# A four-block transformer stack on one core: a new table of stage times and PSUM banks, the instructions unchanged

## The chip, the core and the metric

The kernel runs on one core of a Trainium2 chip. It is a single program for the five engines: TensorE (PE) multiplies matrices and writes PSUM, VectorE (DVE) and ScalarE (ACT) read PSUM and SBUF, GpSimd (POOL) works on SBUF alone, and SyncE (SP) issues the DMAs. The metric is the device time of one execution in microseconds.

## The reference, cut to what matters

The input x is 64 rows of sequences with 64 positions and 128 features, that is 4096 tokens. Eight blocks follow each other, each added to x with a gate of its own:

```python
x = x + tanh(g_xattn[0]) * L0_xattn(ctx, layernorm(x), mask, ...)     # cross attention, 8 heads
x = x + tanh(g_ffn[0])   * L0_ffn(layernorm(x), ...)                  # two layers of local attention + gated MLP
x = x + tanh(g_xattn[1]) * L1_xattn(layernorm(x), ctx, lens, ...)     # linear + decayed "patches"
x = x + tanh(g_ffn[1])   * L1_ffn(layernorm(x), Wg, A, B)             # top 2 of 8 low-rank experts
x = x + tanh(g_xattn[2]) * L2_xattn(ctx, layernorm(x), mask, b)       # attention on given keys and values
x = x + tanh(g_ffn[2])   * L2_ffn(layernorm(x), ...)                  # ternary weights, 8-bit activations
x = x + tanh(g_xattn[3]) * L3_xattn(layernorm(x), ctx, ...)           # attention, 16 heads
x = x + tanh(g_ffn[3])   * L3_ffn(layernorm(x), ...)                  # ternary weights, conv of 3 taps, silu
```

All of it is per sequence, so that a tile of two sequences (128 tokens) goes through the whole stack without any other tile.

## The kernel before, in words

There are 32 tiles of 128 tokens. For one tile the work is a chain of some 250 **stages**, each a few instructions on one engine. A stage's name says where it is: `l0a` is the first cross attention, `l0f0` and `l0f1` the two layers of the first feed-forward block, `l1a`, `l1f`, `l2a`, `l2f`/`l2g`, `l3a` (with two halves `l3a0`, `l3a1`), `l3f`/`l3g` the others. The ending says what it does: on PE `_yt`, `_qt`, `_pt`, `_ot` are transposes, `_sc` scores, `_pv` weights times values, `_out` the last product; on ACT `_exp` is the exponential and `_ht`, `_pts`, `_ots`, `_qts` copy a transposed result from PSUM to SBUF; on DVE `_max` and `_sub` take the row maximum off the scores, `_st`, `_var`, `_eps`, `_y` are a layer norm, `_x` adds a block's result to x; on POOL `_rstd` is the power -1/2.

Several tiles are under way at once: most buffers exist G = 5 times and tile i uses number i mod 5. Each engine is a single queue, so the order in which stages of different tiles follow each other on an engine is fixed when the program is written. That order comes from the **table**. Every stage has a time in tenths of a microsecond; tile i's stage counts as that time plus PERIOD * i, with PERIOD = 489; `in_turn` (line 194) always takes the stage with the smallest such number among the next stages of all tiles:

```python
head = min(left, key=lambda h: (TIMES[h[0]][h[3]] + PERIOD * h[1], h[1]))
```

A tile's own stages on an engine keep their order whatever the table says, and every stage waits on semaphores for its inputs. So the table decides only who stands in front of whom. There are eight lists: PE, ACT, "patch" (two ACT stages, `patch_sq` on line 711 and `patch_power` on line 716), DVE, POOL, "pick" (two POOL stages, `pick_reach` with its powers and compares on lines 504 to 609, and `picks`), SP (the issues of DMAs: `*_dup`, `second`, `first`, `third`, `store`), and "prep" (DVE work on weights in the first tiles).

The second part is the **bank table**. PSUM has eight banks. Each PE stage has a first bank, a number of banks, and the stages that read it. `take` (line 1298) makes a PE stage wait for the readers of whatever lay in its banks before:

```python
for k in range(bank, bank + n):
    for reader, of in held.get(k, ()):
        stage_of(reader, of)
    held[k] = [(reader, i) for reader in readers]
```

`stage_of` (line 1285) leaves a wait out where PE has already waited for a later stage of the same engine, judged by the same table. So the number of waits on PE also follows from the table: writing out both orders gives 2,052 waits on PE before.

ACT loads a table of functions (line 696) whenever the next stage needs another set than the one loaded: the exponential is in one set, Gelu and tanh in the other. With the order before that is 71 loads, two per tile in the steady part.

Lines that the prediction speaks of: PE 1315 (transposes of 128x128, among them `l1f_ot` from `vtmp`, `l2a_yt`, `l0a_yt`), 1322 (four or eight transposes: `l3a0_pt`, `l3a1_pt`, `l3g_qt`), 1336 and 1344 (`l0a_sc`, `l2a_sc`), 1382 (`l0f_qk`), 1388 (`l0f1_v`, `l0f0_v`), 1395 (`l0f_qkt`), 1402 and 1408 (`l0f_sc`), 1455 to 1459 (`l0a_kv`), 1500 (`l1a_out`, second part), 1565 (`l3a_sc`). ACT 711 (`patch_sq`), 739 (`l3g_round` and other roundings), 761 (`l0f_sq`), 785 (`l2g_qts`, `l3g_qts`), 807 (`l1f_tanh`). DVE 989 (`_y`: from `xin` it is `l0a_y`), 1005 and 1008 (`_max`, `_sub`), 1025 (`l1a_x`), 1053 (`l0f_den`), 1059 and 1062 (`l0f_turned`), 1068 (`l0f_qkn`), 1177 (`l1f_o`, writes `vtmp`), 1182 (`l1f_x`), 1219 (`l3a_part`), 1116 (`l0a_st`). POOL 504 (powers and sums), 607 and 609 (`pick_reach`). SP 463 and 464 (`_dup`), 472 and 473 (`second`).

Of the kernel before, what the change touches and what calls it, by code (L numbers as in the profile page):

```python
# [42 lines left out]
PE_TIMES = """
    l0a_kv 695, l0a_yt 695, l0a_q 702, l0a_sc 785, l0a_pt 836, l0a_pv 851, l0a_ot 875, l0a_out 889, l0f0_yt 950,
    l0f0_qk 954, l0f0_v 1107, l0f0_qkt 1121, l0f0_sc 1157, l0f0_pt 1195, l0f0_pv 1244, l0f0_ot 1288, l0f0_wo 1309,
    l0f0_sh 1329, l0f0_lt 1378, l0f0_hid 1405, l0f0_out 1502, l0f1_yt 1521, l0f1_qk 1547, l0f1_v 1551,
    l0f1_qkt 1718, l0f1_sc 1750, l0f1_pt 1777, l0f1_pv 1796, l0f1_ot 1823, l0f1_wo 1844, l0f1_sh 1856, l0f1_lt 1889,
    l0f1_hid 1930, l0f1_out 1946, l1a_yt 2014, l1a_out 2014, l1f_yt 2031, l1f_lg 2047, l1f_ot 2142, l1f_out 2166,
    l2a_yt 2214, l2a_sc 2215, l2a_pt 2252, l2a_pv 2260, l2f_qt 2335, l2f_hid 2356, l2g_qt 2421, l2g_out 2437,
    l3a_yt 2493, l3a_qkv 2493, l3a0_sc 2510, l3a1_sc 2627, l3a0_pt 2658, l3a0_pv 2683, l3a1_pt 2704, l3a1_pv 2727,  # L50
    l3a_tt 2735, l3a_ot 2752, l3a_out 2768, l3f_qt 2835, l3f_hid 2867, l3g_qt 2953, l3g_out 2970
    """
ACT_TIMES = """
    l0a_vs 681, l0a_ht 684, l0a_exp 837, l0a_pts 837, l0a_ots 893, l0f0_hs 931, l0f0_sq 968, l0f0_vs 1112,
    l0f0_qts 1122, l0f0_exp 1170, l0f0_pts 1200, l0f0_ots 1301, l0f0_lts 1389, l0f0_bent 1449, l0f1_hs 1550,
    l0f1_sq 1566, l0f1_vs 1583, l0f1_qts 1727, l0f1_exp 1741, l0f1_pts 1781, l0f1_ots 1825, l0f1_lts 1882,
    l0f1_bent 1937, l1a_ht 2044, l1f_ht 2049, l1f_tanh 2112, l1f_ots 2127, l2a_ht 2203, l2a_exp 2227, l2a_pts 2227,
    l2f_round 2333, l2f_qts 2358, l2f_bent 2369, l2g_round 2391, l2g_qts 2431, l3a_ht 2484, l3a_q 2484, l3a_vs 2497,
    l3a0_exp 2606, l3a0_pts 2650, l3a1_exp 2663, l3a0_os 2687, l3a1_pts 2698, l3a1_os 2709, l3a_ots 2759,
    l3f_round 2825, l3f_qts 2856, l3f_bent 2870, l3g_round 2962, l3g_qts 2962  # L60
    """
# [3 lines left out]
DVE_TIMES = """
    l0a_st 532, l0a_var 575, l0a_eps 587, l0a_y 621, l0a_k 706, l0a_qs 731, l0a_max 792, l0a_sub 796, l0a_inv 868,
    l0a_o 871, l0a_x 886, l0f_st 902, l0f_var 904, l0f_eps 904, l0f_y 936, l0f0_den 1011, l0f0_turned 1026,
    l0f0_qkn 1090, l0f0_max 1136, l0f0_sub 1145, l0f0_inv 1242, l0f0_o 1263, l0f0_y1 1310, l0f0_st 1322,
    l0f0_var 1337, l0f0_eps 1346, l0f0_y 1364, l0f0_gated 1464, l0f0_x 1506, l0f1_den 1584, l0f1_turned 1588,
    l0f1_qkn 1670, l0f1_max 1760, l0f1_sub 1767, l0f1_inv 1791, l0f1_o 1796, l0f1_y1 1856, l0f1_st 1861,  # L70
    l0f1_var 1861, l0f1_eps 1863, l0f1_y 1907, l0f1_gated 1924, l0f1_x 1958, l1a_st 1966, l1a_var 1971,
    l1a_eps 1979, l1a_y 1997, l1a_x 2024, l1f_st 2024, l1f_var 2033, l1f_eps 2054, l1f_lgs 2077, l1f_top 2080,
    l1f_mid 2080, l1f_rest 2093, l1f_sel 2106, l1f_w 2121, l1f_o 2143, l1f_x 2160, l2a_st 2177, l2a_var 2180,
    l2a_eps 2186, l2a_y 2219, l2a_max 2219, l2a_sub 2230, l2a_inv 2262, l2a_o 2262, l2a_x 2265, l2f_st 2285,
    l2f_var 2294, l2f_eps 2301, l2f_y 2302, l2f_abs 2312, l2f_lim 2319, l2f_inv 2327, l2f_step 2362, l2f_pre 2367,
    l2g_abs 2397, l2g_lim 2403, l2g_inv 2406, l2g_step 2435, l2g_x 2453, l3a_st 2457, l3a_var 2467, l3a_eps 2471,
    l3a_y 2483, l3a_part 2495, l3a0_max 2545, l3a0_sub 2551, l3a1_max 2640, l3a1_sub 2685, l3a_inv 2742, l3a_o 2746,
    l3a_x 2769, l3f_st 2778, l3f_var 2787, l3f_eps 2792, l3f_y 2792, l3f_abs 2809, l3f_lim 2826, l3f_inv 2826,
    l3f_step 2830, l3f_q 2835, l3f_act 2896, l3g_abs 2896, l3g_lim 2905, l3g_inv 2931, l3g_step 2931, l3f_x 2976
    """  # L80
# [1641 lines left out]
```

## Time and profile before

| what | value |
|---|---|
| median of 3 runs | 1769.86 us (1769.22 to 1777.59) |
| the profiled execution, its own time | 1784.65 us |
| its span, first to last instruction | 1782.9 us |
| mean granted TensorE clock | 0.928 |
| PE busy | 1443.3 us, 81% |
| DVE busy | 1366.3 us, 77% |
| ACT busy | 980.0 us, 55% |
| POOL busy | 733.6 us, 41% |
| chain that ended last | PE 43%, DVE 30%, ACT 16%, issue 9% |

The chain that ended last goes back from the last instruction to whatever released each step. Its shares say that no engine alone sets the end: the chain changes between PE, DVE and ACT many times in each tile. The program is periodic: after the first four tiles the same sequence of instructions comes back with each tile, about 50 us apart, and so the profile is best read one period at a time, and in differences of period between tiles.

### The profile page before, as it was taken

The numbers are of one execution on the slowest core, as the hardware profiler recorded it, in microseconds if no ns is written. First come the engines' busy times: TensorE is split into PE (matmuls) and PEld (weight loads), VectorE is DVE, ScalarE is ACT, GpSimd is POOL, SyncE is SP. The second block draws the span as 40 slices with busy tenths as digits, with TensorE's granted clock in tenths as the row PEclk, the third lists the DMA queues.
The fourth block names the chain that finished last, engine by engine and source line by source line (L and its number), as shares of the span: only waits on it lengthen the run. The fifth ranks groups of instructions, "written<-read, shape, count | busy, mean of one in ns | idle before, by whom it ended". The sixth has DMA issues, their size and how long they took to land.

```text
span 1782.9 us, 41970 instructions
## 1 busy us (share of the span) xinstructions
PE 1443.3 (81%) x16268; PEld 1022.2 (57%) x16268; DVE 1366.3 (77%) x4055; ACT 980.0 (55%) x1992; POOL 733.6 (41%) x1140
## 2 busy tenths in 40 slices
PE   1567888888888888888888888888888888987775
PEld 1345565566665655666655556666566656665432
DVE  4466687887888888888887888888888888887652
...
DMA packets 130947, 64.34 MB, mean 36 GB/s; under 512 B 97591, under 2 KB 123575, under 8 KB 130494
## 3 DMA queue, kind: packets, MB, share of 16 engines
...
## 4 chain that ended last, share of the span: by engine, by line
PE 43%; DVE 30%; ACT 16%; issue 9%; POOL 1%; POOLq 0%; DVEq 0%; DMA 0%; SPq 0%; ACTq 0%
PE ps_all L1322 9%; DVE mx L1005 4%; PE ps_all L1315 4%; PE ps_all L1440 3%; PE ps_all L1356 3%; ACT wide_b L777 3%; DVE wide_b L1008 2%; ACT L696 2%; PE ps_all L1344 2%; PE ps_all L1426 2%; DVE den L1053 2%; DVE wide_b L1062 2%; PE ps_all L1395 2%; DVE wide_a L1059 2%; DVE small L1032 2%
## 5 line engine op out<-in xcount | busy, mean ns | idle before, releaser
L504 POOL TENSOR_TENSOR rstd<-rstd,minus_half 128x1 f32<-128x1 f32 x320 | 174.9, 550 | 944.3 <-DVE rstd L983 944.2
L1005 DVE TENSOR_REDUCE mx<-ps_all 128x8 f32<-128x1024 f32 (+1 forms) x192 | 165.9, 864 | 152.8 <-PE ps_all L1344 134.3
L504 POOL TENSOR_TENSOR rden<-rden,minus_half 128x16 f32<-128x16 f32 x64 | 188.0, 2937 | 9.7 <-issue 0.4
L504 POOL TENSOR_TENSOR wide_a<-wide_a,wide_b 128x256 f32<-128x256 f32 x256 | 177.5, 724 | 6.4 <-DVE wide_b L1062 6.4
L1322 PE MATMUL ps_all<-ident,wide_b 128*128 128x128 f32 x1024 | 170.6, 308 | 8.1 <-ACT wide_b L746 6.9
L733 ACT COPY wide_a<-ps_all 128x512 f32<-128x512 f32 (+1 forms) x192 | 136.6, 728 | 38.2 <-PE ps_all L1322 26.9
L1322 PEld LDWEIGHTS ps_all<-ident,wide_b 128*128 128x128 f32 x1024 | 143.9, 165 | 12.0 <-ACT wide_b L746 10.2
L733 ACT COPY wide_c<-ps_all 128x512 f32<-128x512 f32 (+1 forms) x96 | 69.9, 728 | 128.1 <-PE ps_all L1322 128.1
L696 ACT ACT_TABLE_LOAD x70 | 89.8, 1283 | 75.2 <-DVE wide_a L1202 47.1
L1382 PE MATMUL ps_all<-w_qkv,ht_shift 128*128 128x512 f32 x256 | 127.4, 622 | 2.2 <-ACT ht_shift L756 2.2
L1008 DVE TENSOR_TENSOR wide_b<-ps_all,mx 128x512 f32<-128x512 f32 (+1 forms) x160 | 125.8, 786 | 1.4
L746 ACT ACTIVATE wide_b<-wide_b 128x512 f32<-128x512 f32 (+1 forms) x160 | 114.6, 716 | 16.0 <-DVE wide_b L1008 11.3
L1440 PE MATMUL ps_all<-ht,w 128*128 128x128 f32 x768 | 99.3, 281 | 0.6 <-ACT ht L731 0.6
L733 ACT COPY ht<-ps_all 128x128 f32<-128x128 f32 x160 | 42.1, 263 | 101.8 <-PE ps_all L1315 100.9
L761 ACT ACTIVATE wide_c<-ps_all 128x1024 f32<-128x1024 f32 x64 | 65.5, 1024 | 55.9 <-PE ps_all L1382 55.9
L1440 PEld LDWEIGHTS ps_all<-ht,w 128*128 128x128 f32 x768 | 95.2, 199 | 0.9 <-issue 0.8
L1609 PE MATMUL ps_all<-w_conv,xt 128*64 128x512 f32 x384 | 94.2, 628 | 0.0
L1097 DVE SCALAR_TENSOR_TENSOR wide_a<-ps_all,b,wide_b 128x128 f32<-128x128 f32 x192 | 55.2, 343 | 50.8 <-ACT wide_b L777 50.8
L1315 PE MATMUL ps_all<-ident,vtmp 128*128 128x128 f32 x128 | 43.7, 341 | 56.9 <-DVE vtmp L1177 43.8
L1388 PE MATMUL ps_all<-w_qkv,ht_shift 128*128 128x512 f32 x128 | 69.2, 625 | 20.4 <-DVE wide_b L1008 20.4
L1068 DVE TENSOR_TENSOR wide_b<-wide_a,rden 128x1024 f32<-128x1024 f32 x64 | 77.9, 1217 | 9.8 <-POOL wide_c L665 6.6
L1053 DVE TENSOR_REDUCE den<-wide_c 128x16 f32<-128x1024 f32 x64 | 77.5, 1212 | 9.1 <-ACT wide_c L761 8.9
...
## 6 DMA issues: line engine op xcount, KB each, us to landing
...
wide_c<-wide_c SPq DMA_DIRECT2D x128, 64.0 KB, 2.3
...
```

Of the source, the lines that this page charges most:

```text
L504: return gp.tensor_tensor(o, a, b, op)
L696: a.preload_act_table_set(name)
L733: a.copy(to, of).then_inc(*done(name))
L746: a.activation(of[:, s, 0:width], of[:, s, 0:width], ACT.Exp, scale=scale).then_inc(*done(f"{n}_exp"))
L1005: v.tensor_reduce(most, of, AX.X, ALU.max).then_inc(*done(f"{n}_max"))
L1008: tt(to, of, bc(most, 3, of.shape[3]), ALU.subtract).then_inc(*done(f"{n}_sub"))
L1053: v.tensor_reduce(den[:, s, :], wide_c[:, s, 0:2 * BANK].rearrange("p (g e) -> p g e", g=16), AX.X, ALU.add).then_inc(*done(f"{n}_den"))
L1315: nc.tensor.transpose(ps(name, 0, P), of, ident[:]).then_inc(*done(name))
L1322: m = nc.tensor.transpose(ps(name, c * P, P), of[:, c * P:c * P + P], ident[:])
L1382: m = mm(ps(f"{n}_qk", q * BANK, BANK), hs, w_qkv[:, L, q * INNER:q * INNER + INNER], start=True, stop=True)
L1440: m = mm(ps(f"{n}_hid", half * BANK + c * P, P), w_1[:, L, half, c, :], ht[:, s, :], start=True, stop=True)
L1609: m = mm(ps_all[64 * b:64 * b + 64, BANKS["l3f_hid"][0], :], xt[:, s, b, tap:tap + ROW], w_conv[:, tap, :], start=False, stop=(tap == 2))
```

## The change

Every number of the eight lists of stage times is new, and so is nearly every bank of the bank table. PERIOD, the names of the stages, their order within a tile, what each stage does, the readers of each PSUM result and the set-up are the same. The parts of the diff that the prediction speaks of:

```diff
 PERIOD = 489
 PE_TIMES = """
-    l0a_kv 695, l0a_yt 695, l0a_q 702, l0a_sc 785, ...
-    l0f1_qk 1547, l0f1_v 1551, l0f1_qkt 1718, ... l1f_yt 2031, l1f_lg 2047, l1f_ot 2142, l1f_out 2166,
-    l2a_yt 2214, ... l3g_qt 2953, l3g_out 2970
+    l0a_kv 711, l0a_yt 780, l0a_q 834, l0a_sc 855, ...
+    l0f1_qk 1609, l0f1_v 1629, l0f1_qkt 1720, ... l1f_yt 2102, l1f_lg 2102, l1f_ot 2188, l1f_out 2196,
+    l2a_yt 2247, ... l3g_qt 3022, l3g_out 3029
 ACT_TIMES = """
-    ... l0f0_sq 968, ... l3g_round 2962, l3g_qts 2962
+    ... l0f0_sq 1042, ... l3g_round 2982, l3g_qts 2999
 PATCH_TIMES = """
-    patch_sq 0, patch_power 1162
+    patch_sq 499, patch_power 1260
 DVE_TIMES = """
-    ... l0a_y 621, ... l0f0_sub 1145, ... l1f_o 2143, ... l3a1_max 2640, l3a1_sub 2685, ...
+    ... l0a_y 812, ... l0f0_sub 1286, ... l1f_o 2248, ... l3a1_max 2752, l3a1_sub 2760, ...
 POOL_TIMES = """
-    l0a_rstd 537, l0a_part 584, ...
+    l0a_rstd 574, l0a_part 698, ...
 PICK_TIMES = """
-    pick_reach 551, picks 1247
+    pick_reach 442, picks 1563
 SP_TIMES = """
-    l0a_dup 733, l0f0_dup 1019, l0f1_dup 1760, second 2219, first 2250, third 2411, store 3003
+    l0a_dup 0, l0f0_dup 459, l0f1_dup 642, second 1295, first 1299, third 1525, store 2202
 BANK_TABLE = """
-l0f1_v 2 1 l0f1_vs
+l0f1_v 5 1 l0f1_vs
-l3a0_sc 1 2 l3a0_sub
+l3a0_sc 3 2 l3a0_sub
-l0a_q 0 1 l0a_qs
+l0a_q 4 1 l0a_qs
 ...
```

Written out with `in_turn`, one period of the new order on PE reads (the number behind a stage is how many tiles back it is; before, `l1f_ot-3` stood in front of `l0a_kv`, `l3g_qt-4` in front of `l0f0_out-1`, and `l0f1_qkt-2` behind `l3a0_pv-4`):

```
l0a_kv l1f_ot-3 l1f_out-3 l3a0_pt-4 l0f1_qkt-2 l3a0_pv-4 l0f0_pt-1 l3a1_pt-4 l2a_yt-3 l0a_yt l2a_sc-3
l3a1_pv-4 l0f0_pv-1 l0a_q l3a_tt-4 l0f1_sc-2 l2a_pt-3 l0a_sc ... l2g_qt-3 l0f0_qk l2g_out-3 l0f1_out-2
l0f0_out-1 l3g_qt-4 l3a_yt-3 l3g_out-4 l3a_qkv-3 l1a_yt-2 l0f1_yt-1 l1a_out-2 l3a0_sc-3 l0f1_qk-1
l1f_yt-2 l1f_lg-2 l0f1_v-1 l0f0_v l0f0_qkt l0f0_sc l3a1_sc-3
```

The part of the order on DVE, before and after:

```
before: l1a_x-2 l1f_st-2 ... l3a0_max-3 l3a0_sub-3 l0f0_qkn l0f1_den-1 l1f_lgs-2 l0f1_turned-1 l1f_top-2
        l1f_mid-2 l0a_y+1 l1f_rest-2 l1f_sel-2 l0f0_max l1f_w-2 l0f0_sub l1f_o-2 l3a1_max-3 l0f1_qkn-1
        l1f_x-2 l0a_k+1 l2a_st-2 l2a_var-2 l2a_eps-2 l3a1_sub-3 l0a_qs+1 l2a_y-2
after:  l1a_x-2 l0a_st+1 l1f_st-2 ... l3a0_max-3 l3a0_sub-3 l0f0_qkn l1f_lgs-2 l0f1_den-1 l1f_top-2
        l0f1_turned-1 l1f_mid-2 l1f_rest-2 l1f_sel-2 l1f_w-2 l0f0_max l1f_o-2 l3a1_max-3 l0f0_sub
        l0f1_qkn-1 l3a1_sub-3 l1f_x-2 l2a_st-2 l2a_var-2 l2a_eps-2 l2a_y-2 l0a_y+1 l0a_k+1
```

With the new order PE has 2,260 waits in place of 2,052, and ACT again 71 table loads.

## Rows read from the trace of the kernel before

**Rows 1.** PE timeline: first instruction of `l0a_kv` in tiles 4, 11, 12, 31.

```profile
211.29 0.32 PE L1455 MATMUL ps_all<-rows,row_sel 128*128 128x128 bf16 x1
...
566.58 0.22 PE L1455 MATMUL ps_all<-rows,row_sel 128*128 128x128 bf16 x1
...
615.13 0.22 PE L1455 MATMUL ps_all<-rows,row_sel 128*128 128x128 bf16 x1
...
1568.77 0.31 PE L1455 MATMUL ps_all<-rows,row_sel 128*128 128x128 bf16 x1
```

**Rows 2.** Windows of PE: stretch, us, PE busy (x), PEclk, DMA share, GB/s.

```profile
566.60:615.10 48.50, 41.52 (x509) 1.00 0.14 37
...
965.00:1016.90 51.90, 44.24 (x509) 0.95 0.13 34
...
611.00:614.90 3.90, 2.02 (x42) 1.00 0.23 55
614.90:619.00 4.10, 4.03 (x22) 0.58 0.04 4
```

**Rows 3.** Who waited for whom, PE alone, whole span: us, times, longest.

```profile
PE ps_all L1315 <- DVE vtmp L1177: 43.8, 31, 3.3
PE ps_all L1402 <- ACT wide_a L733: 41.1, 33, 3.2
PE ps_all L1322 <- ACT wide_c L739: 39.1, 30, 4.7
...
PE ps_all L1388 <- DVE wide_b L1008: 20.4, 28, 0.7
```

**Rows 4.** ACT timeline, 595 to 598 us.

```profile
595.43 1.02 ACT L761 ACTIVATE wide_c<-ps_all 128x1024 f32<-128x1024 f32 x1
...
596.75 0.80 ACT L739 ACTIVATE wide_c<-wide_a,plus_round,small 128x512 f32<-128x512 f32 x1
```

**Rows 5.** DVE timeline, 603 to 620 us.

```profile
603.44 0.35 DVE L1025 SCALAR_TENSOR_TENSOR x<-ps_all,gate,x 128x128 f32<-128x128 f32 x1 [0.44 <-PE ps_all L1500]
...
606.90 1.21 DVE L1068 TENSOR_TENSOR wide_b<-wide_a,rden 128x1024 f32<-128x1024 f32 x1
...
614.02 0.69 DVE L1008 TENSOR_TENSOR wide_b<-ps_all,mx 128x512 f32<-128x512 f32 x1
614.63 0.28 DVE L1177 TENSOR_TENSOR vtmp<-ps_all,weight 128x128 f32<-128x128 f32 x1
614.83 1.21 DVE L1005 TENSOR_REDUCE mx<-ps_all 128x8 f32<-128x1024 f32 x1
615.96 1.22 DVE L1068 TENSOR_TENSOR wide_b<-wide_a,rden 128x1024 f32<-128x1024 f32 x1
617.52 0.29 DVE L1182 TENSOR_TENSOR x<-ps_all,x 128x128 f32<-128x128 f32 x1 [0.34 <-PE ps_all L1513]
...
618.59 1.22 DVE L1008 TENSOR_TENSOR wide_a<-ps_all,mx 128x1024 f32<-128x1024 f32 x1
```

**Rows 6.** POOL timeline: tile 0, then 602 to 616 us.

```profile
27.86 0.56 POOL L504 TENSOR_TENSOR rstd<-rstd,minus_half 128x1 f32<-128x1 f32 x1 [11.43 <-DVE rstd L983]
39.34 0.19 POOL L504 TENSOR_TENSOR ctx_rms<-ctx_sq,ln_eps 128x1 f32<-128x1 f32 x1 [10.92 <-DMA plug<-plug_dram]
...
41.48 1.19 POOL L504 TENSOR_TENSOR wide_a<-ot,part 128x256 f32<-128x256 f32 x2
...
602.48 2.77 POOL L504 TENSOR_TENSOR wide_a<-wide_a,wide_b 128x256 f32<-128x256 f32 x4 [0.25 <-DVE wide_b L1062]
...
612.65 2.77 POOL L504 TENSOR_TENSOR wide_a<-wide_a,wide_b 128x256 f32<-128x256 f32 x4
```

**Rows 7.** Timelines of PE and DVE in tile 0.

```profile
42.77 0.58 PE L1336 MATMUL ps_all<-rows,row_sel 128*128 128x256 bf16 x2 [12.21 <-POOL wide_a L504]
...
30.59 0.35 DVE L1128 SCALAR_TENSOR_TENSOR qt<-ps_all,b_q,mask_row 128x128 f32<-128x128 f32 x1 [0.66 <-PE ps_all L1465]
```

**Rows 8.** Chain that ended last, 158 to 170 us.

```profile
162.72 2.72 DMA v_pair<-in_v
```

More of the change, by code:

```diff
@@ L43 @@
 PE_TIMES = """
[L44 to L48, printed above, removed]
@@ L49 @@
-    l2a_yt 2214, l2a_sc 2215, l2a_pt 2252, l2a_pv 2260, l2f_qt 2335, l2f_hid 2356, l2g_qt 2421, l2g_out 2437,
-    l3a_yt 2493, l3a_qkv 2493, l3a0_sc 2510, l3a1_sc 2627, l3a0_pt 2658, l3a0_pv 2683, l3a1_pt 2704, l3a1_pv 2727,
-    l3a_tt 2735, l3a_ot 2752, l3a_out 2768, l3f_qt 2835, l3f_hid 2867, l3g_qt 2953, l3g_out 2970
+    l0a_kv 711, l0a_yt 780, l0a_q 834, l0a_sc 855, l0a_pt 907, l0a_pv 914, l0a_ot 931, l0a_out 940, l0f0_yt 1016,
+    l0f0_qk 1030, l0f0_v 1149, l0f0_qkt 1163, l0f0_sc 1163, l0f0_pt 1243, l0f0_pv 1303, l0f0_ot 1359, l0f0_wo 1379,
@@ new lines @@
+    l0f0_sh 1401, l0f0_lt 1465, l0f0_hid 1495, l0f0_out 1548, l0f1_yt 1573, l0f1_qk 1609, l0f1_v 1629,
+    l0f1_qkt 1720, l0f1_sc 1819, l0f1_pt 1860, l0f1_pv 1879, l0f1_ot 1889, l0f1_wo 1897, l0f1_sh 1917, l0f1_lt 1977,
+    l0f1_hid 1995, l0f1_out 2035, l1a_yt 2058, l1a_out 2065, l1f_yt 2102, l1f_lg 2102, l1f_ot 2188, l1f_out 2196,
+    l2a_yt 2247, l2a_sc 2268, l2a_pt 2321, l2a_pv 2344, l2f_qt 2399, l2f_hid 2431, l2g_qt 2494, l2g_out 2520,
+    l3a_yt 2539, l3a_qkv 2545, l3a0_sc 2564, l3a1_sc 2658, l3a0_pt 2693, l3a0_pv 2706, l3a1_pt 2712, l3a1_pv 2760,
@@ L52 @@
+    l3a_tt 2791, l3a_ot 2852, l3a_out 2863, l3f_qt 2896, l3f_hid 2941, l3g_qt 3022, l3g_out 3029
     """
 ACT_TIMES = """
[L54 to L57, printed above, removed]
@@ L61 @@
     """
 PATCH_TIMES = """
-    patch_sq 0, patch_power 1162
+    patch_sq 499, patch_power 1260
     """
 DVE_TIMES = """
[L66 to L79, printed above, removed]
+    l0a_st 652, l0a_var 667, l0a_eps 673, l0a_y 812, l0a_k 818, l0a_qs 838, l0a_max 868, l0a_sub 872, l0a_inv 947,
@@ new lines @@
+    l0a_o 953, l0a_x 973, l0f_st 976, l0f_var 990, l0f_eps 996, l0f_y 1000, l0f0_den 1105, l0f0_turned 1115,
+    l0f0_qkn 1193, l0f0_max 1264, l0f0_sub 1286, l0f0_inv 1327, l0f0_o 1327, l0f0_y1 1385, l0f0_st 1405,
+    l0f0_var 1425, l0f0_eps 1447, l0f0_y 1461, l0f0_gated 1526, l0f0_x 1571, l0f1_den 1695, l0f1_turned 1709,
+    l0f1_qkn 1778, l0f1_max 1817, l0f1_sub 1839, l0f1_inv 1885, l0f1_o 1885, l0f1_y1 1943, l0f1_st 1951,
+    l0f1_var 1951, l0f1_eps 1954, l0f1_y 1962, l0f1_gated 2039, l0f1_x 2054, l1a_st 2054, l1a_var 2054,
@@ L80 @@
+    l3a_y 2550, l3a_part 2583, l3a0_max 2627, l3a0_sub 2644, l3a1_max 2752, l3a1_sub 2760, l3a_inv 2796, l3a_o 2821,
+    l3a_x 2865, l3f_st 2865, l3f_var 2869, l3f_eps 2883, l3f_y 2883, l3f_abs 2908, l3f_lim 2910, l3f_inv 2917,
+    l3f_step 2917, l3f_q 2923, l3f_act 2970, l3g_abs 2970, l3g_lim 2970, l3g_inv 3000, l3g_step 3024, l3f_x 3082
     """
 POOL_TIMES = """
-    l0a_rstd 537, l0a_part 584, l0f_rstd 920, l0f0n_rstd 999, l0f0_rot 1005, l0f0_one 1019, l0f0_rstd 1215,
-    l0f1n_rstd 1534, l0f1_rot 1538, l0f1_one 1560, l0f1_rstd 1890, l1a_rstd 1960, l1f_rstd 1995, l2a_rstd 2040,
```

117 lines of the change are left out of this document (64 added, 53 removed).

## The prediction

> **What bounds the kernel now.** I read the chain that ended last first: it is spread over PE, DVE and ACT, with no engine at its limit. So the period is what to read. The first instruction of `l0a_kv` stands at 211.29 us for tile 4 and at 1568.77 for tile 31 [rows 1]: 1357.5 us for 27 periods, 50.28 each. But single periods differ: tile 11 takes 48.55 (566.58 to 615.13) [rows 1], tile 19 takes 51.9. The windows of these two tiles show what differs: in the short one the granted clock is 1.00 and PE is busy 41.52 us, in the long one 0.95 and 44.24, with the same 509 matmuls [rows 2]. So the time has two parts. At full clock a period is 48.55, of which PE is idle about 7. And the lower clock costs on average 50.28 - 48.55 = 1.73 per period, 47 us over 27.
>
> Where PE idles is in its waits: 43.8 us in 31 waits of `l1f_ot` for `l1f_o` on DVE, 41.1 of `l0f_sc` for a copy on ACT, 39.1 in 30 waits of `l3g_qt` for `l3g_round` on ACT, 20.4 in 28 waits of `l0f1_v` for `l3a0_sub`, which still reads its PSUM bank [rows 3]. Where the clock falls: from 611.0 to 614.9 PE works 2.02 of 3.90 us, around the waits of `l0f0_sc` and `l1f_ot`; in the next 4.1 us the mean grant is 0.58, mostly the lower of the two levels, 1.2 in place of 2.4 GHz [rows 2]. Those two waits are paid twice, once as idle time and once as slow matmuls of `l0a_kv` and `l3a0_pt` behind them.
>
> **The change, part by part.** No instruction is added, removed or resized, and ACT's table loads stay 71. All effects are of order. I follow one full-clock period (tile 11's) in the new order.
>
> *`l3g_round`.* Before, ACT did `l0f0_sq` (1.02 us) and `patch_sq` in front of it, and it began at 596.75 [rows 4]. Now both stand behind it or elsewhere (`patch_sq` in front of `l3f_bent`), so it can begin at 595.43, 1.3 earlier, and `l0f0_out` fills PE in front of `l3g_qt`. The 39.1 us of that wait go. But `l1a_x`, the next place where the chain passes to DVE, is also held by `l0f0_turned` and `l3a_part` on DVE. I carry 0.5 of the 1.3: `l1a_x` at 602.9 in place of 603.44 [rows 5]. The price is that `l0f0_sq` comes later by `l3g_round` less what is saved, some 0.4, and `l0f0_den` and POOL's `l0f0_rot` some 0.5 later. `l0f0_rot` ended at 602.48 + 2.77 = 605.25 and `l0f0_qkn` began at 606.90 [rows 5, 6]: 1.65 of slack hide it. Without that slack the whole DVE stretch would move by 0.5.
>
> *`l0f1_v`.* Its bank is 5 in place of 2 and no longer that of `l3a0_sc`. The 0.7 wait goes, but `l1f_lg` now follows `l1f_yt` with nothing between, and waits for the copy of `l1f_ht`, about 0.45 (14.4 of 20.4 given back). DVE is later than PE here: I count nothing.
>
> *The DVE stretch.* From `l1a_x` (603.44) to `l1f_o` (614.63 + 0.28) DVE never idles for more than a semaphore's delay [rows 5]. The new order takes `l0a_y` out, puts `l0a_st`, of about the same length, in, and moves `l0f0_sub` (0.61) behind `l1f_o`. With the 0.5 from above `l1f_o` starts at 614.63 - 0.5 - 0.6 = 613.5.
>
> *`l0a_kv` in front of `l1f_ot`.* It depends on nothing late and puts 1.0 us of matmuls into the 1.4 us wait. `l1f_ot` is then free by 1.0 or so earlier and `l0a_kv` is already done, so PE reaches `l3a0_pt` up to 2 us earlier.
>
> *What is late next.* `l0f1_qkt` now stands in front of `l3a0_pv`, `l0f0_pt`, `l3a1_pt` and `l2a_yt`, and waits for `l0f1_qkn`. On DVE that comes after `l3a1_max` (1.13 start to start) and `l0f0_sub` (0.61) behind `l1f_o` (0.2): start 613.5 + 1.9 = 615.4, end 616.6, if POOL's `l0f1_rot`, which ended at 612.65 + 2.77 = 615.42 [rows 6], comes no later. It was 615.96 + 1.22 = 617.2 [rows 5]. PE would wait some 0.3 there. `l3a1_sub` ends at 617.8 in place of 619.8, so `l3a1` gains 2; but `l1f_x` is behind it, at 617.7 in place of 617.52 [rows 5], and `l2a_y` ends only 0.4 earlier, since `l3a1_sub` no longer stands in its way. `l2a_yt` and its copy let `l2a_sc` start some 0.9 earlier. Behind it PE is dense, and walking on through `l0f0_wo`, `l0a_pv` and `l3f_hid` I keep 0.7 at `l0f1_hid`, where the period closes. `l0a_yt` and `l0a_q` are later by 3 us or more than before, but `l0a_sc`, whose inputs had long been there, keeps its place.
>
> So **0.7 per period** at full clock; from tile 0's set-up to the end I count 31 periods: -22 us. Bounds: nothing, and the two waits entirely recovered (43.8 + 39.1 = 83). I take the walk because it names what holds each step.
>
> *The clock.* The low clock costs 47 us and follows the stretch with `l0f0_sc` and `l1f_ot`; half of its idle time goes, since `l0a_kv` fills it. The 1.2 wait of `l0f0_sc` stays. Bounds: 0 and 47; I take a third, -15. The Trainium skill (TensorE: Matmul & The Clock Gate, A second HAM failure mode: psum-queue depth-cycling) says that frequent short idle times between groups of matmuls alone make the clock swing, and speaks against this gain: the order keeps several. By it the term would be 0, the forecast 15 us later.
>
> *PE waits.* 208 more. A stage with one wait starts 0.05 after its releaser, one with more 0.14 (`l1f_o` ended at 614.91 [rows 5], `l1f_ot` began 0.06 later). At 0.09 each that is 19 us if all were on the path; most stand where PE is dense and the wait long met. I take +3, bounds 0 and 19.
>
> *Start.* `pick_reach` now stands in front of `l0a_rstd` on POOL. In tile 0 it waited for the plug's DMA until 39.34, and `l0a_part` (41.48) stood behind it; `l0a_rstd` had run at 27.86 [rows 6]. Now the chain from `l0a_rstd` (27.86) to the end of `l0a_qs` (30.59 + 0.35) [rows 6, 7] starts at 41.5: `l0a_sc` at 44.7 in place of 42.77 [rows 7], +1.9. In return `second` of tile 0 is issued ahead of two other entries of SP and the 2.72 us in which the chain stood on its DMA [rows 8] can shrink: -1. In the steady part SP's queue is reordered too (`l0f1_dup` in front of `second`, `store` and `first`), but `second` still lands some 8 us before `l2a_sc`, and `first` a whole period early: nothing, and if that cover went, up to 2.72 per tile.
>
> Sum: -22 - 15 + 3 + 1.9 - 1 = -33. On the profiled execution 1784.65 - 33 = 1751.6. That execution was 15 us over the median of the runs shown, so on the median 1769.86 - 33 = **1737**.
>
> **The rivals.** A measurement tells this kernel from no change from about 0.5%, 9 us.
>
> *Both waits come back nearly whole (0.15).* The waits of `l1f_ot` and `l3g_qt` are on the chain in most tiles. If 1.2 per period is kept and two thirds of the clock's cost: -37 - 31 = -68, 1702. Against it is DVE's slack-free stretch.
>
> *Nothing moves (0.12).* DVE's stretch and its POOL chain (`l0f1_den`, power, `l0f1_rot`, `l0f1_qkn`) set the period, and PE's idle time reappears at `l0f1_qkt`. For it: PERIOD is the same 48.9 us in both tables, and the program runs at 48.55 where the clock is full. The time is then 1769.86 + 3 + 0.9, less a few us of the clock's cost: 1770.
>
> *Slower by the clock (0.14).* The mechanism: PE now has short waits at `l0f0_sc`, `l1f_out` (for `l1f_ots`), `l0f1_qkt` and `l3a1_pt` within 10 us. If the clock falls in every period as long as in tile 19's, a period costs 51.9 - 50.28 = 1.6 more; less the 0.7, +0.9 or 29 us: 1799. It decides from the point where the low clock costs over 1.73 + 0.7 = 2.4 per period. For it: tile 11 paid nothing and tile 19 2.7 us of busy time (44.24 against 41.52) [rows 2], so the cost is not at its worst now.
>
> **How the numbers follow.** The forecast has 0.59, with its own range 1717 to 1757 (clock term 0 to two thirds, waits 0 to 8, schedule 0.4 to 1.0). The range reaches to the strong case below and past no change above: 1702 to 1776; outside are most of the slow case and half of the strong one. Faster: 0.59 + 0.15 = 0.74. Same: 0.12. Slower: 0.14.
>
> **What would show it.** Right: full-clock periods of 47.6 to 48.2; no wait of line 1315 on `vtmp` before `l0a_kv`, the wait of line 1322 on line 739 near zero; a wait of line 1395 on line 1068 of 0.1 to 0.5 per tile in their place; `l0a_sc` of tile 0 near 44.7; mean granted clock over 0.928. Wrong: line 1395's wait at 1 us or more (DVE stretch bounds), or a mean clock under 0.92 with the 509 matmuls busy for over 44 us per period.

## The result and the profile after

The changed kernel takes 1759.88 us (median of 11 runs, 1748.43 to 1765.57), the kernel before in the same comparison 1775.88 (11 runs, 1769.22 to 1781.7): a ratio of 0.9902, 95% interval 0.9877 to 0.9926. So it is faster by 1.0%, 16 us, where 33 were forecast. The direction is right, but the size is half of what was forecast, and the time lies inside the wide range (1702 to 1776) but 3 us over the forecast's own (1717 to 1757). The two profiled executions differ by more, 1784.65 and 1754.01, because the one of before lies 9 us over its median and the one of the changed kernel 6 under. I use the traces for durations and order, and the medians for sums.

The page of the changed kernel:

```profile
span 1752.3 us, 42083 instructions
...
PE 1460.1 (83%) x16268; PEld 993.7 (57%) x16268; DVE 1371.4 (78%) x4055; ACT 967.1 (55%) x1992; POOL 741.9 (42%) x1140
...
PEclk9778999999999999899999998999899899998875
...
DVE 36%; PE 33%; ACT 12%; POOL 9%; issue 8%; POOLq 2%; DVEq 0%
```

The first instruction of `l0a_kv` in tiles 4, 12, 13 and 31, as [rows 1] has them (PE timeline):

```profile
210.26 0.23 PE L1455 MATMUL ps_all<-rows,row_sel 128*128 128x128 bf16 x1
...
606.62 0.23 PE L1455 MATMUL ps_all<-rows,row_sel 128*128 128x128 bf16 x1
...
653.96 0.23 PE L1455 MATMUL ps_all<-rows,row_sel 128*128 128x128 bf16 x1
...
1537.65 0.29 PE L1455 MATMUL ps_all<-rows,row_sel 128*128 128x128 bf16 x1
```

A period at full clock is 653.96 - 606.62 = 47.34 us. It was 48.55, so the schedule gained 1.2 per period. The mean of 27 is (1537.65 - 210.26) / 27 = 49.16: the lower clock costs 1.82 per period in this execution, where it cost 1.73 in the other. Windows of a full-clock period, of one with falls, and of the fall in it (columns: stretch, us, then busy (x) of PE, weight loads, DVE, ACT and POOL, PEclk, DMA share, GB/s):

```profile
606.60:653.90 47.30, 41.86 (x512) 28.92 (x508) 41.61 (x126) 29.83 (x63) 21.37 (x33) 1.00 0.15 39
...
554.40:606.60 52.20, 47.71 (x512) 32.79 (x508) 41.98 (x126) 29.66 (x63) 24.02 (x37) 0.87 0.13 34
...
595.30:602.10 6.80, 6.45 (x12) 2.85 (x12) 5.61 (x10) 1.19 (x2) 5.01 (x10) 0.50 0.00 0
```

The same 512 matmuls take 5.9 us more in the second period. The fall (0.50, the lower of the two levels) lies 41 us into the period; before, it lay behind `l0f0_sc` and `l1f_ot`, where the period begins [rows 2]. In front of it PE waits 1.32 us with `l3a0_sc`, and within it 0.35 with `l1f_lg`:

```profile
593.58 1.09 PE L1565 MATMUL ps_all<-wide_a,qt 32*64 32x512 f32 x8 [1.32 <-DVE wide_a L1219]
```

In the 27 periods the clock falls 21 times: 14 falls begin 37 to 41 us into the period, 7 at 47 us, and they last 3.4, 6.8 or 10.2 us, 126 in all. The two waits are new in PE's list (lines 1565 and 1507):

```profile
PE ps_all L1565 <- DVE wide_a L1219: 39.4, 30, 1.3
PE ps_all L1402 <- DVE wide_b L1062: 38.4, 25, 3.6
...
PE ps_all L1395 <- DVE wide_b L1068: 14.3, 5, 8.7
...
PE ps_all L1507 <- DVE wide_b L1008: 12.4, 16, 2.4
...
PE ps_all L1322 <- ACT wide_c L739: 6.3, 3, 4.7
...
PE ps_all L1315 <- DVE vtmp L1177: 4.3, 2, 3.3
```

The two waits that were to go are gone (43.8 and 39.1 in [rows 3]). In their place 39.4 us stand in front of `l3a0_sc` (for `l3a_part`), 1.3 each. The wait of `l0f0_sc` stays, as forecast, but is mostly for another releaser: 38.4 us in 25 waits, 1.5 each, for `l0f1_turned`, which still reads its PSUM bank, in place of 1.2 each for ACT's copy [rows 3]. In sum PE idles less in a full-clock period than before, 47.30 - 41.86 = 5.4 us in place of 7.0 [rows 2].

### The profile page after: what moved, and what is told of

Same layout as the page of the kernel before. It is cut to its first block, busy times and chain, and to the rows that moved or that the text cites. A ratio compares the mean times of both kernels' runs of the same rounds, so it can differ in the third digit from the quotient of the medians.

```text
span 1752.3 us, 42083 instructions
## 1 busy us (share of the span) xinstructions
PE 1460.1 (83%) x16268; PEld 993.7 (57%) x16268; DVE 1371.4 (78%) x4055; ACT 967.1 (55%) x1992; POOL 741.9 (42%) x1140
## 4 chain that ended last, share of the span: by engine, by line
DVE 36%; PE 33%; ACT 12%; POOL 9%; issue 8%; POOLq 2%; DVEq 0%
PE ps_all L1609 5%; POOL rden L504 4%; DVE mx L1005 4%; POOL wide_a L504 3%; DVE wide_b L1008 3%; ACT wide_a L733 3%; PE ps_all L1382 3%; PE ps_all L1565 3%; DVE wide_b L1068 3%; DVE wide_a L1097 2%; DVE wide_b L1062 2%; PE ps_all L1408 2%; DVE wide_a L1059 2%; DVE stats L974 2%; PE ps_all L1322 2%
## 5 line engine op out<-in xcount | busy, mean ns | idle before, releaser
L504 POOL TENSOR_TENSOR rstd<-rstd,minus_half 128x1 f32<-128x1 f32 x320 | 178.7, 558 | 793.8 <-DVE rstd L983 793.8
L1322 PE MATMUL ps_all<-ident,wide_b 128*128 128x128 f32 x1024 | 171.1, 299 | 17.0 <-ACT wide_b L746 9.7
L1382 PE MATMUL ps_all<-w_qkv,ht_shift 128*128 128x512 f32 x256 | 149.9, 716 | 2.2 <-ACT ht_shift L756 2.2
L1322 PEld LDWEIGHTS ps_all<-ident,wide_b 128*128 128x128 f32 x1024 | 121.0, 150 | 47.9 <-DVE wide_b L1019 14.9
L1565 PE MATMUL ps_all<-wide_a,qt 32*64 32x512 f32 x512 | 72.5, 647 | 40.0 <-DVE wide_a L1219 39.4
L1395 PEld LDWEIGHTS ps_all<-ident,wide_b 128*128 128x128 f32 x512 | 67.0, 157 | 42.4 <-issue 42.4
L1395 PE MATMUL ps_all<-ident,wide_b 128*128 128x128 f32 x512 | 76.0, 298 | 16.8 <-DVE wide_b L1068 14.3
L1382 PEld LDWEIGHTS ps_all<-w_qkv,ht_shift 128*128 128x128 f32 x256 | 49.7, 215 | 67.2 <-issue 67.2
```

The costliest lines, as they stand in the source:

```text
L504: return gp.tensor_tensor(o, a, b, op)
L1322: m = nc.tensor.transpose(ps(name, c * P, P), of[:, c * P:c * P + P], ident[:])
L1382: m = mm(ps(f"{n}_qk", q * BANK, BANK), hs, w_qkv[:, L, q * INNER:q * INNER + INNER], start=True, stop=True)
L1395: m = nc.tensor.transpose(ps(f"{n}_qkt", c * P, P), wide_b[:, s, c * P:c * P + P], ident[:])
L1565: n_mm = mm(ps_all[64 * b:64 * b + 64, bank + m, :], qt[r, s, 64 * b:64 * b + 64], k_part[r, s, b * BANK:b * BANK + BANK], start=True, sto ...
```

## The experiments

Table edits are written as stage and time. "Filled" kernels have matmuls of 512 bf16 columns whose products nothing reads, just ahead of a wait of PE and in a PSUM bank that is free there. They depend on nothing late, so they keep PE busy and should leave the schedule alone.

**1. `l0a_kv` in front of `l1f_ot`, alone, in the kernel before.**

```diff
-l1f_ot 2142
+l1f_ot 2163
```

> The kernel before with one swap on PE: l0a_kv and l0a_yt in front of l1f_ot. Theory (the gain is spread over the whole order, since the chain changes between engines): l3a1_max on DVE ends when it did, so the full-clock period, 48.55 us, falls by 0 to 0.5 us, the 43.8 us of waits of l1f_ot vanish and PE waits elsewhere; the time stays within 0.5% of the kernel before. Rival (the wait was on the path and is simply recovered): 1.0 us less per period, 47.5 us, 30 us in all, ratio 0.983.

(`l0a_yt`, with the same time as `l0a_kv`, moves with it.) Measured 1810.08, ratio 1.0212 (1.0177 to 1.0247). Both readings missed. PE's list has a wait that neither foresaw:

```profile
PE ps_all L1455 <- issue: 41.4, 29, 2.4
```

In the old bank table `l0a_kv` shares a bank with `l1f_lg`, which `l1f_o` reads last. Placed earlier, it waits for the very stage whose wait it was to fill. Order and banks are one design.

**2. `l3g_round` and `l0f0_out` early, alone, in the kernel before.**

```diff
-patch_sq 0, l3g_round 2962, l0f0_out 1502
+patch_sq 420, l3g_round 2922, l0f0_out 1485
```

> The kernel before with patch_sq moved in front of l3f_bent, l3g_round in front of l0f0_sq, and l0f0_out in front of l3g_qt. Theory of the prediction: l1a_x comes 0.5 us earlier and the full-clock period falls from 48.55 to about 48.05, ratio 0.99 if the clock's cost stays 1.7 per period. Rival (the step needs the bank and DVE changes of the full table): the period stays within 0.15 of 48.55.

Measured 1786.26, ratio 1.0081 (1.005 to 1.0112): slower, although the wait went. I took its shortest period, 48.14, for its full-clock period. Experiment 13 shows that this was wrong, and that the rival of this experiment holds.

**3 to 6. Fillers: both kernels filled, then each filler alone in the changed one.**

```diff
+for _ in range(4): mm(ps("l1a_out"), ones3, rows[:, 0:BANK], start=True, stop=True)
+if L == 0:
+    for _ in range(4): mm(ps("l0f0_v"), ones3, rows[:, 0:BANK], start=True, stop=True)
```

(The first is at the head of `l1a_out` and in its bank; PE's wait is that of the next stage, `l3a0_sc`. The second is at the head of `l0f0_sc`, in the bank of `l0f0_v`. The kernel before has three at `l0f0_sc` and five at `l1f_ot`, in its bank.)

> The changed kernel with idle time of PE filled by matmuls whose result is never read: four of 512 bf16 columns at the head of l1a_out (ahead of the 1.3 us wait of l3a0_sc) and four behind l0f0_qkt (in the 1.5 us wait of l0f0_sc), in PSUM banks that are free then. Theory (the lower clock follows stretches in which PE idles, and its cost, not the order, ate the forecast): granted clock rises from 0.923 to 0.96 or more, most periods are 47.3 to 47.8 us, the time falls 15 to 45 us under the changed kernel, ratio to before 0.965 to 0.982. Rival A (the clock falls for another reason, such as the mix of matmuls): clock 0.92 to 0.93, ratio 0.99 or above because the fillers only cost. Rival B (the filling delays l1a_out or l0f0_sc): full-clock period over 48.

> The kernel before with idle time of PE filled in the same way: three matmuls of 512 bf16 columns behind l0f0_qkt and five in front of the wait of l1f_ot. Theory: the low clock at l0a_kv and l3a0_pt goes in most periods, granted clock 0.95 or more, full-clock period stays 48.55, time 15 to 45 us less, ratio 0.975 to 0.992. Rival (another cause of the low clock): clock 0.92 to 0.935, ratio 1.00 or more.

> The changed kernel with only the second filler: four matmuls of 512 bf16 columns behind l0f0_qkt, in the wait of l0f0_sc. If each stretch of idle PE time brings on its own fall of the clock just behind it, this takes away the low clock that begins at 47 us of the period and leaves the one at 37 to 41, whose idle time is that in front of l3a0_sc: clock 0.94 to 0.95, ratio to before about 0.975. If the two work together, either filler alone brings nearly the whole 52 us: ratio under 0.97.

> The changed kernel with only the first filler: four matmuls at the head of l1a_out, ahead of the wait of l3a0_sc. If each stretch of idle time brings on its own fall, the low clock at 37 to 41 us of the period goes and the one at 47 stays: clock 0.94 to 0.95, ratio to before about 0.975, full-clock period 47.3. If l0f0_sc's wait alone decides: ratio 0.985 to 0.99, no gain.

Changed kernel, both: **1707.99**, 0.9643 (0.9615 to 0.967), granted clock 0.961 in place of 0.923. Before, filled: 1745.9, 0.9856 (0.9824 to 0.9888), clock 0.963. `l0f0_sc` alone: 1732.18, 0.9733 (0.9664 to 0.9802). `l1a_out` alone: 1722.45, 0.9696 (0.9662 to 0.9729). The theory held in both filled kernels; in the changed one the gain was more than its 15 to 45 us. The falls in the two traces with one filler show what each filler does. The one at `l0f0_sc` takes away those at 47 us of the period and leaves nine at 37 to 38; so the first reading of its run held there. The one at `l1a_out` leaves none at 37 to 41 and three at 47 to 50, so it acts on both. The gains of 28 and 37 us are no sum for the 52 of both together, and the first is loose, since its four runs spread from 1720.83 to 1747.72. The windows over 27 periods, of the changed kernel filled and of the kernel before filled:

```profile
209.20:1495.50 1286.30, 1173.41 (x13882) 799.91 (x13932) 1125.96 (x3376) 806.24 (x1675) 612.80 (x920) 1.00 0.15 37
```

```profile
209.40:1530.90 1321.50, 1173.68 (x13880) 809.44 (x13933) 1120.89 (x3376) 816.07 (x1672) 607.70 (x919) 1.00 0.14 36
```

The mean periods are 1286.3 / 27 = 47.64 and 48.94, close to the full-clock ones, which fillers left at 47.34 and 48.56. The two filled kernels differ by 37.9 us, and 1.22 x 31 is 38: with the clock's cost removed the schedule's gain stands whole. The fillers recover 30 us before (1775.88 to 1745.9) and 52 after (1759.88 to 1707.99). So the clock's bill grew by 22, and -38 + 22 is the -16 measured. The two traces, with 1.73 and 1.82 per period, hide this growth, since their executions lie on opposite sides of their medians. What fillers recover is a lower bound of a bill, as 0.3 to 0.4 per period is left. The Trainium skill (TensorE: Matmul & The Clock Gate, A second HAM failure mode: psum-queue depth-cycling) has short idle times between groups of matmuls make the clock swing. These runs agree: the clock fell 21 times in 27 periods of the changed kernel, and once when eight matmuls filled about half of two idle times of 1.3 and 1.5 us (20 us are left of 39.4 at `l3a0_sc`, 21 of 46.8 at `l0f0_sc`).

**7. The new times with the old banks.** (The table of banks is the one of before.)

> The new stage times with the banks of before (2,059 waits on PE, as before). If the order alone brings the gain, the full-clock period is 47.3 us as in the changed kernel and the time is within 0.5% of it (0.99 of before). If times and banks belong together, l0a_kv (bank 3) waits for l1f_o, which reads l1f_lg in bank 3, as in the run with l0a_kv moved alone, and other stages wait in the same way: full-clock period over 49.5, ratio 1.01 or more. I expect the second.

Measured 1942.66, ratio 1.094 (1.0911 to 1.0968), a full-clock period of 54.7: times and banks belong together, and by more than expected. Bank waits spread over many stages. Of these three the first and the last are such; the middle one is the wait for ACT's copy that was there before [rows 3]:

```profile
PE ps_all L1315 <- DVE ot L1091: 46.6, 33, 2.0
PE ps_all L1402 <- ACT wide_a L733: 38.2, 32, 1.2
PE ps_all L1583 <- DVE ot L1124: 37.8, 27, 1.9
```

The reverse, old times with new banks, would have a stage wait for one queued behind it, and wasn't tried.

**8 to 10. The one swap undone, unfilled and filled; and a lengthened DVE stretch.**

```diff
-l1f_ot 2188
+l1f_ot 2177
```

> The changed kernel with l1f_ot back in front of l0a_kv, as before. Theory of the prediction (l0a_kv fills a wait): l1f_ot waits about 0.4 us for l1f_o behind l3a1_sc, and l0a_kv, l3a0_pt and the rest stand behind it, but DVE (l3a1_max to l3a1_sub) is later anyway: full-clock period 47.3 to 47.6. Rival (PE is on the path there): 47.34 plus the wait, 47.8 or more. The time rises by 0 to 15 us over the changed kernel's 1760, more of it by the clock than by the period.

> The changed kernel with l1f_ot back in front of l0a_kv (as in the run before, 1725.57) and both fillers of four matmuls (as in the run of 1707.99). Two readings of the 34 us that this one swap gave. If the swap only moved and shortened the stretches at the lower clock (the full-clock period of that run was 47.5, not shorter than 47.34), it gives back nothing that the fillers don't give already: clock near 0.96, period 47.5 at full clock, 1710 to 1716, some 4 us (0.13 to 0.16 per period of 31) above the run with the fillers alone. If the swap shortens the path itself, the two gains add: below 1695.

```diff
+if n == "l1f":
+    for k in range(2): ts(tick[:, 2 * i + k:2 * i + k + 1], mv[:, s, 1:2], eps, None, ALU.add)
```

> The changed kernel with two more DVE instructions of 128x1 in every tile, written to a tile of their own that nothing reads, in front of l1f_eps, in the middle of the dense DVE stretch. They lengthen the full-clock period by about as much as the swap of l1f_ot and l0a_kv did (47.34 to 47.5) and leave every order as it is. Theory that the order of the two matmul stages made the swap 34 us faster: this run is 3 to 6 us slower than the changed kernel (1763 to 1766) with a granted clock of 0.92 to 0.925. Rival, that the place at which the clock falls hangs on the period's length or on such small shifts, whatever makes them: clock of 0.935 or more and a time of 1725 to 1745.

With `l1f_ot` back in front of `l0a_kv` the changed kernel takes 1725.57, ratio 0.9713 (0.9685 to 0.9742): 34 us **less** than as changed, where 0 to 15 more were expected. Filled it takes 1708.69, 0.9636 (0.9606 to 0.9667), no other than experiment 3, with full-clock periods of 47.33. So the swap is worth nothing in the schedule and costs 34 us in the clock. PE's waits at `l3a0_sc` and `l0f0_sc` are as long as in the changed kernel (39.3 us in 30, 47.6 in 31), that at `l1f_lg` nearly so; but 14 of the 20 falls in 27 periods now come 47 us into the period, and all but one last 3.4 us, 72 us in all where it was 126. One of them:

```profile
1129.30:1132.70 3.40, 3.40 (x19) 3.10 (x16) 3.24 (x5) 2.31 (x6) 1.97 (x4) 0.51 0.65 167
```

The two added DVE instructions gave 1749.17, 0.986 (0.9818 to 0.9902), clock 0.922 in the profiled execution. That lies between the two readings, 11 us under the median of the changed kernel where the theory had 3 to 6 over and the rival 15 to 35 under. The trace has no fewer falls than the changed kernel (28, 140 us in all); its shortest period is 47.45 and the mean 1.9 more. So a small shift moves the time by some us, but did not bring the 34. Why the order with `l1f_ot` first has the shorter falls stays open.

**11. `l3a_part` in front of `l0f0_turned`.**

```diff
-l3a_part 2583
+l3a_part 2581
```

> The changed kernel with l3a_part in front of l0f0_turned on DVE (time 2583 to 2581), so that the 1.3 us wait of l3a0_sc for l3a_part (39.4 us in 30 waits) goes. l3a0_max, behind it on DVE, is not earlier, since DVE is dense there. Theory (schedule on DVE, PE's idle stretches costly by the clock alone): full-clock period 47.3 to 47.6, the wait gone from PE's list but 0.5 to 1.3 us of PE idle time back at l1f_lg or l1f_out; clock 0.925 to 0.945 and 1735 to 1757. Rival (the wait of l3a0_sc is on the path): full-clock period below 46.8, time below 1735. Other rival (l0f0_turned later by 0.6 delays POOL's l0f0_rot and with it l0f0_qkn, which has 0.7 of slack): period 47.9 or more, 1770 or more.

Measured 1796.27, ratio 1.013 (1.0091 to 1.0168), full-clock period 48.53. The third reading had the size, but not the cause: `l0f0_qkn` waits for POOL no more than before. DVE's list has a new wait, for ACT's copy into `qt`:

```profile
DVE wide_a L1219 <- ACT qt L827: 34.8, 32, 3.6
```

The slack of 1.3 that `l3a_part` showed existed only because `l0f0_turned` (2.4 us) stood before it. One microsecond of idle DVE there costs 1.2 of period. Nor did the wait in front of `l3a0_sc` go. It grew, and is now for `l0f0_turned`, which reads bank 4, one of the two that the new table gives to `l3a0_sc`:

```profile
PE ps_all L1565 <- DVE wide_b L1062: 72.9, 29, 2.6
```

**12. `pick_reach` behind `l0a_rstd` again, unfilled and filled.**

```diff
-pick_reach 442
+pick_reach 584
```

> The changed kernel with POOL's pick_reach behind l0a_rstd again (time 442 to 584), everything else as changed. It measures the term for the start alone: l0a_sc of tile 0 from 43.91 back to 42.8, tile 4 some 1 us earlier, and nothing in the steady part, where pick_reach of a later tile waits for nothing: 1758 to 1760. Rival: in the steady part l0a_rstd stands in front of the pick and l0a_y earlier changes nothing, but picks come later, bound l1a_out and cost up to 1 us per period: 1775 or more.

> The changed kernel with pick_reach behind l0a_rstd (the run of 1787.3 us) and the two fillers of four matmuls. If the 27 us that this order cost were the clock's alone (its full-clock period was 47.47), it stands with the other filled kernels: clock 0.955 or more, full-clock period 47.3 to 47.5, 1706 to 1716. If the order costs on POOL or DVE as well: full-clock periods over 47.6 and 1725 or more.

Measured 1787.3, ratio 1.007 (1.004 to 1.0099), and filled 1791.54, 1.0087 (1.0058 to 1.0116): fillers don't help. The filled trace still has 21 falls in 27 periods, now 5 to 7 us into the period, where no filler stands, and its full-clock periods are longer as well. At the start `l0a_sc` of tile 0 is back at 42.5 from 43.9, as expected, but the steady part is slower. POOL and then DVE in the filled kernel:

```profile
608.76 0.90 POOL L504 TENSOR_TENSOR ctx_rms<-ctx_sq,ln_eps 128x1 f32<-128x1 f32 x1
...
612.84 0.26 POOL L654 TENSOR_SCALAR rden<-den 128x16 f32<-128x16 f32 x1
613.25 2.94 POOL L504 TENSOR_TENSOR rden<-rden,minus_half 128x16 f32<-128x16 f32 x1
616.15 2.78 POOL L504 TENSOR_TENSOR wide_a<-wide_a,wide_b 128x256 f32<-128x256 f32 x4
```

```profile
619.04 1.22 DVE L1068 TENSOR_TENSOR wide_b<-wide_a,rden 128x1024 f32<-128x1024 f32 x1 [1.75 <-POOL wide_c L665]
```

`pick_reach` (from 608.76) and `picks` both stand ahead of `l0f1n_rstd` and `l0f1_rot`, and `l0f1_qkn` on DVE waits 1.75 us for them; full-clock periods are 49.18. Part of this, 0.7 us, is the first instruction's own: it takes 0.90 where the same one took 0.19 in [rows 6]. It began while `l0f0_qkn` ran on DVE (608.40 to 609.61), and ended just behind it. Unfilled, the shortest was 47.47, so I had taken its loss for the clock's. Each period under 47.7 of the unfilled kernel stands right behind one of over 52, so that such a period only gives back a part of what the one before lost.

**13. The step of experiment 2 in the filled kernel before.**

> The kernel before with l3g_round in front of l0f0_sq and patch_sq, l0f0_out in front of l3g_qt (alone 1786, its full-clock period 48.14 against 48.56), and the fillers of the filled kernel before (3 in front of l0f0_sc, 5 in front of l1f_ot; alone 1745.9). With the clock's cost removed the schedule is what is left: 0.42 per period x 31 = 13 us less, 1733 (1729 to 1739). Rival, that this order brings idle stretches of its own at places the fillers don't cover: clock below 0.955, 1745 or more.

Measured 1753.5, ratio 0.9864 (0.9815 to 0.9913), 8 us more than the filled kernel before, with full-clock periods of 48.43 to 48.54: the step brings 0.1, and the rival is right that it has falls of its own, in 7 of 27 periods with these fillers. Unfilled (2) its mean period was 50.52, so its bill there is 2.1 per period: the gain is smaller than what the clock took. The DVE timeline shows why, at the place where I let it carry 0.5:

```profile
838.22 0.35 DVE L1025 SCALAR_TENSOR_TENSOR x<-ps_all,gate,x 128x128 f32<-128x128 f32 x1 [0.44 <-PE ps_all L1504]
```

`l1a_x` waits 0.44 for `l1a_out`, as before [rows 5]. Removing the wait at `l3g_qt` did not bring it earlier against DVE's stretch.

**14. `l0f0_sub` back in front of `l1f_o`, filled.**

```diff
-l0f0_sub 1286
+l0f0_sub 1268
```

> The changed kernel with l0f0_sub back in front of l1f_o and l3a1_max on DVE, and the two fillers. The forecast let l1f_o start 0.6 earlier by this swap. Theory (DVE has no idle time from there to l3a1_sub, so only the order of its parts changes): full-clock period within 0.15 of 47.34 and 1706 to 1713; l1f_ot later by 0.6 and its wait longer, covered behind it. Rival (the 0.6 is on the path by l1f_ot, l1f_x, l2a_y): full-clock period 47.7 to 48.0, 1719 to 1728.

Measured 1706.43, ratio 0.9606 (0.9571 to 0.9641), full-clock period 47.30: this swap is worth nothing either.

**15. Three short DVE stages back inside the dense stretch, filled.**

```diff
-l0a_y 812, l0f0_x 1571, l3a_y 2550
+l0a_y 739, l0f0_x 1600, l3a_y 2573
```

> The changed kernel with both fillers and three DVE stages back where the kernel before had them, inside the dense stretch from l0f0_den to l0f1_qkn: l3a_y and l0f0_x behind l0f0_den, l0a_y of the next tile between l1f_mid and l1f_rest. Theory (the period is set by that stretch, so what was moved out of it is gained whole): the stages take 0.25, 0.20 and 0.25 from start to start, 0.7 together, so the full-clock period is 47.34 + 0.7 = 48.0 (47.8 to 48.2) and the time 1708 + 0.7 x 31 = 1730 (1723 to 1736). Rival (the stretch isn't the bound, POOL's chain l0f0n_rstd to l0f1_rot or PE is): full-clock period within 0.2 of 47.34, 1705 to 1714.

Measured 1724.79, ratio 0.9691 (0.9644 to 0.9738), full-clock period 47.78: 17 us over the filled kernel and 0.44 of 0.7 per period. So the period follows the stretch, but by less than was put in; what takes up the rest was not looked for.

**16 and 17. `l1f_sel`, in the filled kernel before.** It lasted 0.75 before and 0.23 after, at the same size. DVE and POOL in the changed kernel, and DVE in the kernel before:

```profile
652.51 0.23 DVE L1169 TENSOR_SCALAR rest<-rest,small 128x8 f32<-128x8 f32 x1
...
652.91 1.42 POOL L504 TENSOR_TENSOR wide_a<-wide_a,wide_b 128x256 f32<-128x256 f32 x2
```

```profile
612.65 0.75 DVE L1169 TENSOR_SCALAR rest<-rest,small 128x8 f32<-128x8 f32 x1
...
613.92 0.16 DVE L1174 SCALAR_TENSOR_TENSOR weight<-weight,rest 128x8 f32<-128x8 f32 x1
```

Before, it starts at 612.65 with POOL's `l0f1_rot` [rows 6]; after, it is done when POOL starts.

```diff
-l0a_y 621
+l0a_y 648   (16)
+l0a_y 688   (17)
```

> The kernel before with its fillers (3 and 5; alone 1745.9, full-clock period 48.56) and l0a_y behind l0f0_max in place of in front of l1f_rest on DVE. In the kernel before l1f_sel (128x8) lasts 0.75 us in nearly every tile, and l0f1_rot starts on POOL in the same 0.01 us; in the changed kernel it lasts 0.23 and POOL's start falls elsewhere. With l0a_y out of its way it starts 0.25 earlier. Theory (the start of l0f1_rot on POOL stretches a DVE instruction that starts with it): l1f_sel 0.23, full-clock period 48.56 - 0.5 = 48.05, 1746 - 0.5 x 31 = 1730 (1725 to 1737). First rival: the stretch hits the instruction that now runs there (l0f0_max over 0.69), and the period stays 48.5, 1741 to 1750. Second rival: l1f_sel is shorter but the path is elsewhere: same time, l0f0_max 0.69.

> The kernel before with its fillers (3 and 5; alone 1745.9, full-clock period 48.56) and l0a_y between l3a1_max and l0f1_qkn on DVE. In the run with l0a_y behind l0f0_max the stretch went from l1f_sel to l0a_y (0.86 in place of 0.34) and l1f_w (0.70 in place of 0.16), both started while POOL worked on one of the four instructions of l0f1_rot, each 0.69 long, and both ended just behind that instruction's end; instructions that read PSUM in the same stretch (l0f0_max, l0f0_sub, l1f_o, l3a1_max) kept their length. Theory (a DVE instruction with all its operands in SBUF that starts inside one of POOL's waits for its end): l1f_sel 0.23, since it starts before l0f1_rot; l1f_w starts at about 0.65 after POOL's start, close to the end of the first instruction, and lasts 0.3 or less; l0a_y starts behind l0f1_rot and lasts 0.34. Full-clock period 48.56 - 0.5 = 48.05 (47.95 to 48.2), time 1730 (1724 to 1737). Rival (something else in the order holds the path): l1f_sel is short and the period 48.4 or more, 1741 or more.

16 took 1765.22, ratio 0.9946 (0.992 to 0.9972), 19 us **more** than the filled kernel before, and more than any of the three readings had. The first rival's cause is near, though it is not `l0f0_max` that is hit:

```profile
651.03 0.23 DVE L1169 TENSOR_SCALAR rest<-rest,small 128x8 f32<-128x8 f32 x1
651.18 0.69 DVE L1005 TENSOR_REDUCE mx<-ps_all 128x8 f32<-128x512 f32 x1
651.79 0.86 DVE L989 TENSOR_SCALAR y<-xin,mv,rstd 128x128 f32<-128x128 f32 x1
652.57 0.70 DVE L1174 SCALAR_TENSOR_TENSOR weight<-weight,rest 128x8 f32<-128x8 f32 x1
...
651.16 2.78 POOL L504 TENSOR_TENSOR wide_a<-wide_a,wide_b 128x256 f32<-128x256 f32 x4
```

`l0a_y` takes 0.86 in place of 0.34 and `l1f_w` 0.70 in place of 0.16, both while POOL works. 17 moved `l0a_y` behind POOL's work: **1730.39**, ratio 0.9752 (0.9712 to 0.9792), 15.5 us less than the filled kernel before, as the theory had it; its full-clock periods are 48.2 to 48.3, a little over the 48.05 expected.

## Why the prediction was wrong in its size

*The clock term* (-15) is the step that failed. It said that the low clock follows the stretch with `l0f0_sc` and `l1f_ot`, that half of the stretch's idle time goes since `l0a_kv` fills it, and that a third of the cost goes with it; its bounds, gains of 0 and 47, left no room for a loss. The runs show the bill grown from 30 to 52 us (3 to 6), +22. The swap that was to bring the gain is what loses it in the changed kernel. With it undone, the full-clock period is the same (9) and the bill is 1725.57 - 1708.69 = 17 us: 13 under that of before, near the forecast -15. With it, the bill is 52. The wait of `l3a0_sc`, which the walk didn't name, is new, and the falls moved behind it. But idle time alone doesn't give the bill: PE idles 1.5 us less in a full-clock period than before (5.4 for 7.0), and the 34 us come with waits as long. The reading of the Trainium skill gave 0 here, nearer, but still short. The rival "slower by the clock" had the right mechanism, that the low clock can take back the gain, though with other waits; it took 0.7 of 1.22 per period. Of the signs named, the granted clock over 0.928 did not come (0.923 in the profiled execution); in 6 of the 11 runs it lay under 0.92, one half of the sign of being wrong.

*The schedule term* (-22, 0.7 per period) was right in sign and undersized: 1.22 per period, -38, over its own range of 0.4 to 1.0. That the sum stayed inside the wide range is luck, since the two errors (-16 and +37) have opposite signs. And three of the steps it was walked from bring 0.1 or nothing: `l3g_round` (carried 0.5; 13), `l0f0_sub` behind `l1f_o` (0.6; 14), and `l0a_kv` in front of `l1f_ot` (8 and 9). The walk named DVE's stretch as slack-free and then carried gains of PE and ACT into it. What the runs show is that the stretch itself became shorter. From `l0f0_den` to `l0f1_qkn` it takes 16.9 us in place of 18.4 (start to start on DVE's timeline, full-clock periods). Of the 1.22, about 0.44 are the three short stages moved to where DVE is idle (15). Another 0.4 to 0.5 is the stretching of `l1f_sel` by POOL (17: 15.5 us over 31 tiles, and full-clock periods shorter by 0.4), which the walk read as that instruction's length. The last 0.3 or so were not tried apart. The 0.44 wait at `l1a_x` [rows 5], which the changed kernel doesn't have, may be among them, and so may a second stretched instruction. In the trace of before `l2a_y` lasts 0.61 in 27 tiles, begun while POOL ran `l0a_part`; in the changed kernel it lasts 0.35:

```profile
570.99 0.61 DVE L989 TENSOR_SCALAR y<-x,mv,rstd 128x128 f32<-128x128 f32 x1
```

*PE waits* (+3): not seen apart; the match of 37.9 with 38 leaves little room. *Start* (+1.9): `l0a_sc` of tile 0 at 43.91 for 44.7, +1.1; the -1 for `second` was not measured. That `pick_reach` costs nothing in the steady part was right only because it left POOL's chain as `picks` came in (12). *What is late next:* `l0f1_qkt` hardly waits (14.3 us in 5 waits, 8.7 of it one). POOL's `l0f1_rot` ends 0.14 us before `l0f1_qkn` starts, so it stands close behind as the next bound; no run tried that.

*The base:* the difference was taken against a median of 3 runs; over 11 it is 1775.88, 6 us higher.
